# Expert attention on one core: scores in row tiles, maxima on the whole array, keys padded by TensorE, and one unused matmul per unit

## The reference

```python
sx = jnp.einsum('bsh,ndh->bnsd', x, hl_w) + hl_b[None, :, None, :]
q = jnp.einsum('bnsd,neod->bneso', sx, wq)
k = jnp.einsum('bnsd,nod->bnso', sx, wk)
v = jnp.einsum('bnsd,nod->bnso', sx, wv)
scores = jnp.einsum('bnesd,bntd->bnest', q, k) * d ** 0.5 + causal
att = jax.nn.softmax(scores, axis=-1)
qkv = jnp.einsum('bnest,bntd->bnesd', att, v)
```

## Time and profile before

| | |
|---|---|
| median of 3 runs | 1997.99 us (1995.75 to 2002.71) |
| the profiled execution's own time | 2006.71 us |
| its span, first to last instruction | 2004.9 us |
| mean granted TensorE clock | 0.865 |
| busy: PE, PEld, DVE | 86%, 67%, 74% |
| busy: ACT, POOL | 38%, 34% |
| expert attention, first set-up instruction to the last row's update of the stream | 557 us to about 1382 us |
| a turn of its loop (one row, four units) | 24.2 us from 897.34 to 921.53 us |

### The profile page before, as it was taken

The page is one execution under the profiler, slowest core; times in us unless marked ns, Lnnn a source line. Parts: engine busy times, 40 slices in busy tenths (PEclk is TensorE's granted clock), DMA queues, the critical chain, the costliest instruction groups (busy, mean ns, idle before and its releaser), DMA issues. The chain is left out here.

```text
span 2004.9 us, 45616 instructions
## 1 busy us (share of the span) xinstructions
PE 1719.6 (86%) x15064; PEld 1344.4 (67%) x15064; DVE 1488.5 (74%) x4423; ACT 756.6 (38%) x2274; POOL 690.5 (34%) x957
## 2 busy tenths in 40 slices
PE   1499999999769999999999999973999999788887
PEld 1266666666557777777777777752888888677776
DVE  6166676666627898888889888875766665688887
ACT  2245454545324444344344444321222222343442
POOL 2622222222134555545545445532211111322221
PEclk9999999999869999999999999985555555788788
DMA  2000000000000000000000000000000000000000
GB/s 114 1 2 0 0 0 0 0 0 0 1 1 1 1 2 0 0 0 0 0 0 0 0 0 0 1 1 0 1 0 0 0 0 1 1 5 8 4 6 11
DMA packets 6980, 8.13 MB, mean 4 GB/s; under 512 B 6272, under 2 KB 6272, under 8 KB 6784
## 3 DMA queue, kind: packets, MB, share of 16 engines
q1 hardware_dynamic: 6912, 7.25, 1.1%
HBM read 5.71 MB, written 1.54 MB: 4 GB/s over the span
## 5 line engine op out<-in xcount | busy, mean ns | idle before, releaser
L1142 ACT ACTIVATE ex_pT<-ex_T 128x376 f32<-128x376 f32 (+1 forms) x384 | 162.8, 440 | 217.1 <-PE ex_T L1044 207.9
L604 ACT ACTIVATE al_prob<-al_S,al_negmax 94x94 f32<-94x94 f32 (+1 forms) x512 | 146.2, 375 | 180.0 <-DVE al_negmax L731 180.0
L1207 DVE TENSOR_REDUCE ex_negmax<-ex_R 94x2 bf16<-94x376 f32 (+1 forms) x384 | 186.8, 543 | 30.6 <-PE ex_R L1015 30.0
L1044 PE MATMUL ex_T<-ex_qm,ex_kpad 128*128 128x188 f32 x1024 | 189.7, 329 | 0.0
L505 PE MATMUL al_S<-al_kpad,al_qT 128*94 128x376 f32 x384 | 166.5, 516 | 0.0
L1044 PEld LDWEIGHTS ex_T<-ex_qm,ex_kpad 128*128 128x128 f32 x1024 | 163.0, 192 | 5.1
L944 POOL TENSOR_SCALAR_AFFINE_SELECT ex_pT<-ex_pT 128x512 f32<-128x512 f32 x128 | 84.3, 659 | 236.5 <-ACT ex_pT L1142 236.5
L682 POOL TENSOR_TENSOR al_kpad<-al_kT,al_quad_mask 128x1504 f32<-128x1504 f32 x32 | 86.2, 2692 | 186.3 <-ACTq L619 186.3
L731 DVE TENSOR_REDUCE al_negmax<-al_S 94x2 f32<-94x376 f32 (+1 forms) x192 | 99.1, 542 | 62.6 <-PE al_S L506 56.7
L1554 POOL TENSOR_TENSOR ta_kk<-ta_ext 94x320 f32<-94x320 f32 x64 | 60.4, 961 | 246.4 <-DVE ta_qkn L1734 163.0
L1027 PE MATMUL ex_R<-ex_sxT,wsb 128*128 128x188 f32 x256 | 72.3, 364 | 47.5 <-DVE ex_negmax L1207 47.5
(11 more groups left out here) (308 smaller groups left out, 4300.8 us busy)
## 6 DMA issues: line engine op xcount, KB each, us to landing
tok_xin<-x_t SPq DMA_DIRECT2D x4, 760.0 KB, 6.9
wsb<-weights SPq DMA_DIRECT2D x1, 2531.0 KB, 14.2
out<-stream SPq DMA_DIRECT2D x16, 94.0 KB
tok_par<-tok_w SPq DMA_DIRECT2D x1, 4.5 KB, 1.7
```

Source lines behind the costliest of these rows:

```text
L604: last = nc.scalar.activation(p[:, k, cols], S[0:P, k, cols], ACT.Exp, bias=negmax[g % 2][:, m:m + 1])
L1044: last = nc.tensor.matmul(T[:, k, (j % 2) * N:(j % 2 + 1) * N], kpad[par][:, j, 0:K0], qm[e % 2][:], start=True, stop=True)
L1142: nc.scalar.activation(pT[e % 2][rows, k, cols], T[rows, k, cols], ACT.Exp)\
L1207: red(dst, src, AX.X, ALU.max, negate=True).then_inc(sem["r_used"], 1)
```

## The change

All of it is in `expert_attention`. It has these parts.

1. **Scores in row tiles.** `scores` no longer reads padded keys. Each head's matmul uses only its own 32 rows of the array (`tile_position=(32 * n, 0)`), and each head has a bank of `T`, which has four banks now. It is called for heads 0 and 1 and then for heads 2 and 3, and ACT takes one exponential for each pair (2 x 248 elements, `PAIR`) where it took three.
2. **Maxima on the whole array.** `max_scores` takes 128 and 60 queries in place of 94 and 94. The first 128 need keys 0 to 127 only; the last 60 stand twice, in two column tiles of 64, two heads each. `R` has two banks, and `maxima` is two reductions (512 and 376 elements) instead of three of 376. It is issued for the unit after next, where it was for the next.
3. **Queries in T.** `queries` accumulates in bank 0 of `T` (`QCOL`).
4. **Padded keys by PE.** POOL's `kpad` and `kpadb` go; `kpadb` is made by four more matmuls per row with padded weights `ewkb` (two fills, `kb01` and `kb23`), copied out by ACT.
5. **One unused matmul per unit.** `keep_busy(FILLERS)` multiplies 128 x 128 by 128 x 512 in bf16 into `R` before `max_scores`, and nobody reads it; ahead of units 0, 8 and 20 of the run there are 16 more.
6. **Order.** The order of `FILLS` changes, `fg` standing before `sx` now; DVE's body is reordered, with `maxima(rf, 1)`, `mask_values(ru, 2)` and the gate's softmax at its end; POOL's set-up has 34 operations where it had 21.

```diff
+    WARM, WARM_AT = 16, (0, 8, 20)
+    FILLERS = 1
...
-        FILLS = [("xT", FRONT), ("znT", MLP), ("sx", FRONT), ("k", FRONT), ("fc1", MLP), ("pickA", TAIL),
-                 ("fg", LAST), ("q01", FRONT), ("pickB", TAIL), ("q23", FRONT), ("v", FRONT), ("fc2", MLP)]
+        FILLS = [("xT", FRONT), ("znT", MLP), ("fg", LAST), ("sx", FRONT),
+                 ("pickA", TAIL), ("kb01", FRONT), ("kb23", FRONT), ("q01", FRONT),
+                 ("pickB", TAIL), ("fc1", MLP), ("k", FRONT),
+                 ("q23", FRONT), ("v", FRONT), ("fc2", MLP)]
...
-                    if e == 1 and valid(r):
-                        pool.wait_ge(sem["kT_ready"], r + 1)
-                        for dst in (kpadb, kpad):
-                            nc.gpsimd.tensor_tensor(dst[1 - u][:], kT[:].unsqueeze(1).broadcast_to([128, NH, N]),
...
+            def padded_keys(which):
+                return [(X[:, i * N:(i + 1) * N], ewkb[:, n, :], sxb[:]) for i, n in enumerate(which)]
+            def keep_busy(n):
+
+                for _ in range(n):
+                    nc.tensor.matmul(R[:, 0, :], w_parts[:, 0, 0:128], w_parts[:, 0, 128:640], start=True, stop=True)
...
+                need(pe, sem["r_used"], 2 * u)
+                if isinstance(u, int) and u in WARM_AT:
+                    keep_busy(WARM)
+                keep_busy(FILLERS)
+                early = R[:, 0, :].rearrange("p (n s) -> p n s", n=NH)
+                nc.tensor.matmul(early, qTb[par][:, e, 0:K0], kpadb[par][:, :, 0:K0], start=True, stop=False)
+                nc.tensor.matmul(early, eye[:], maskA[:].unsqueeze(1).broadcast_to([128, NH, K0]), start=False, stop=True)\
+                    .then_inc(sem["r_full"], 1)
+                late = R[:, 1, 0:PAIRED * N].rearrange("p (j s) -> p j s", j=PAIRED)
+                for c in range(2):
+                    nc.tensor.matmul(late[QB * c:QB * c + QB], qTb[par][:, e, K0:NP], kpadb[par][:, c::2, :],
+                                     start=True, stop=False, tile_position=(0, QB * c), skip_group_check=True)
...
-                        if k < 2:
-                            last = nc.tensor.matmul(T[:, k, (j % 2) * N:(j % 2 + 1) * N], kpad[par][:, j, 0:K0],
-                                                    qm[e % 2][:], start=True, stop=True)
...
+                for s in range(2):
+                    for n in heads:
+                        rows = slice(32 * n, 32 * n + 32)
+                        if s == 0:
+                            last = nc.tensor.matmul(T[:, n, 0:N], kT[par][rows, 0:K0], qm[e % 2][rows, :], start=True,
+                                                    stop=True, tile_position=(32 * n, 0), skip_group_check=True)
...
+                nc.scalar.activation(pT[e % 2][:, 2:4, :], T[:, 2:4, 0:PAIR], ACT.Exp).then_inc(sem["tB_used"], 1)
...
+                        ins = nc.scalar.activation(pT[e % 2][:, 0:2, :], T[:, 0:2, 0:PAIR], ACT.Exp)
```

More of the change, by code:

```diff
@@ L1032, in queries, with scores @@
-                last.then_inc(sem["m_full"], 1)
-            def scores(r, par, e):
+                for c in range(2):
+                    last = nc.tensor.matmul(T[:, 0, QCOL + K0:QCOL + N], negmaxB[e % 2][:, 32 - 32 * c:160 - 32 * c],
+                                            eye[:, QB * c:QB * c + K1], start=False, stop=True, skip_group_check=True)
+                return last
+            def scores(r, par, e, heads):
                 u = r * NE + e
                 if e == 0:
-                    pe.wait_ge(sem["kpad_ready"], 2 * r + 2)
+                    pe.wait_ge(sem["k_used"], r + 1)
@@ L1039, in scores @@
                 pe.wait_ge(sem["m_used"], u + 1)
[L1040 to L1049 removed]
+                if heads[0] == 0:
+                    pe.wait_ge(sem["tA_used"], u + 1)
+                else:
+                    need(pe, sem["tB_used"], u)
@@ new lines, in scores @@
+                for s in range(2):
[4 more added lines that the diff above has]
+                                                    stop=True, tile_position=(32 * n, 0), skip_group_check=True)
+                        else:
+                            last = nc.tensor.matmul(T[:, n, N:PAIR], kT[par][rows, QB:NP], qm[e % 2][rows, K0:N],
+                                                    start=True, stop=True, tile_position=(32 * n, 0),
+                                                    skip_group_check=True)
@@ L1108, in body @@
                         fill(t, "sx", [(X[:, 0:N], w("hl_t", C), xT[:])])
-                    if e == 1 and valid(rt):
-                        pe.wait_ge(sem["o_used"], NE * (rt + 1))
-                        fill(t, "pickA", picks(odd, slice(0, P)))
-                    if e == 2 and valid(rt):
-                        fill(t, "pickB", picks(odd, slice(P, N)))
+                    if e == 1 and valid(rf):
+                        fill(t, "q01", projections((0, 1)))
+                    if e == 2 and valid(rf):
+                        fill(t, "k", [(X[:, 0:N], w("ewk"), sxT[odd][:, 0:N])])
                     if e == 3 and valid(rm):
@@ new lines, in body @@
+                    if e == 0 and valid(rf):
+                        act.wait_ge(sem["sx_full"], rf + 1)
+                        need(act, sem["o_used"], NE * (rf - 1))
+                        for dst in (sxT[odd][:, 0:N], sxb[:]):
+                            used("sx_used", dst, ALL, slice(0, N), ACT.Identity, bias=w("hl_bt"))
+                    if e == 1 and valid(rf):
+                        act.wait_ge(sem["q01_full"], rf + 1)
+                        used("q01_used", qTb[odd][:, 0:2, 0:N], ALL, slice(0, 2 * N))
@@ L1334, in body @@
                     link(tt(row_halves(rl), row_halves(rl), fout[:], ALU.add))
+                if valid(rf):
+                    maxima(rf, 1)
                 if valid(ru):
                     mask_values(ru, 2, par)
+                if valid(rt):
+                    dve.wait_ge(sem["gexp_ready"], rt + 1)
+                    flat = gate_exp[:].rearrange("p h n e -> p (h n) e")
+                    link(red(top[:], flat, AX.X, ALU.add))
+                    link(nc.vector.reciprocal(top[:], top[:]))
+                    tt(gate[:].rearrange("p h n e -> p (h n) e"), flat,
+                       top[:].unsqueeze(2).broadcast_to([P, HALVES * NH, NE]), ALU.mult).then_inc(sem["gs_ready"], 1)
             dve.wait_ge(sem["consts"], CONSTS)
```

371 lines of the change are left out of this document (180 added, 191 removed).

## The result

The changed kernel takes 2037.8 us (median of 4 runs, 2034.0 to 2045.4), the kernel before 1999.9 beside it: ratio 1.020, 95% interval 1.016 to 1.023, so it is slower, by about 2%. The profiled execution took 2039.1 us, its span 2037.1. The forecast was 2015, a loss of 17 us.

The account below looks back on a forecast made before the run. The bound was taken to be the loop of dependences through PE, DVE and POOL, not one engine. 2006.7 + 16 (steady rows) + 1 (ends) = 2024 us profiled, 8.7 less for the median: 2015, range 1945 to 2050.

Parts of the forecast that it names:

- Scores: PE's scores of one unit in row tiles: 1.0 us instead of 1.92, bounds 0.70 and 1.92.
- The stall at line 1271: DVE's small `tensor_scalar`, 3.22 us until POOL's padding ends: falls to 0.2 us, DVE gains 3.0 us per row.
- The loop of a row: Dependences from POOL's mixing round to the next, through DVE and PE: 23.0 us against 24.1.
- step 1: DVE ends softmax, POOL mixes, DVE sums, does `maxima(2)`, mask and gate operations; PE's `sx` waits for this: 5.0 us.
- steps 2 and 3: PE's `sx`, scores, `pickA` until DVE reads it, 2.4 us; then DVE's pick through PE's maxima to `pickB`, 5.1 us.
- Step 3: DVE picks, PE waits before `kb01`, then maxima, `weigh`, `q01`, scores, `pickB` and hops: 5.1 us.
- Step 4: `queries`, exponential, POOL's masks and power: 5.2 us with hops; DVE's own path about 4 us, so DVE waits for POOL.
- 4 and 5: The loop's last two parts: `queries` through POOL's power, 5.2 us; DVE from normalisation through `maxima(1)` and a mask, 5.3 us.
- The clock: Steady rows: PE idles at waits and the granted clock dips to 0.88, adding 1.6 us per row; chance 0.45.
- The sum: Some 26 steady rows +16 us, ends +1, on 2006.7: 2024 profiled, 8.7 less for the median, 2015 us.
- the ends: POOL's set-up +4.6 us, three bursts +5, first six rows -9: together +1, within 8 either way.
- The rival on the other side: Clock stays full through the unused matmul and bursts: loop 23.0 us, 1970 us, bounds 1950 to 1992; chance 0.36.

Follow-up runs that it names:

- e7: Kernel before the change, with POOL's padding of the keys cut to two columns: 1987 us.
- e6: Changed kernel without its three bursts of 16 unused matmuls, with ten more unused matmuls per row where TensorE waits for VectorE: 1954.9 us.
- e3: Changed kernel with ten more unused matmuls per row inside TensorE's waits (before xT, sx and kb01), bursts kept: 1964.5 us.
- e10: e6 with four unused matmuls ahead of each unit's maxima (16 per row) and none in the waits: 2012 us.
- e11: e6 with its ten unused matmuls in the waits but none ahead of the units' maxima: 1955 us.
- e12: e6 with the ten unused matmuls in the waits using 32 of the array's 128 rows, same 512 columns: 2016.7 us.
- e13: e6 with one more VectorE multiplication of z by norm_g per row, right behind the first one, on the loop: 35 us slower.

## Why the prediction came out as it did

- **Scores** (taken 1.0, bounds 0.70 and 1.92): 0.70, the lower bound; two pairs run as close as four tiles. By the TensorE page of the Trainium skill ("TensorE: Matmul & The Clock Gate", Part 3) the estimate was 1.92 / 3.07 = 0.63; the trace shows 1.92 / 0.70 = 2.7 times.
- **The stall at line 1271**: gone, 0.17 us. That DVE gains these 3 us and the row doesn't, as forecast ("it doesn't, because of what is behind what"), e7 shows from the other side.
- **The loop of a row**: 23.0 forecast, 22.4 with scores of 0.70, 22.1 measured in e6. Step by step it was 5.0, 2.4, 5.1, 5.2, 5.3 against 5.2, 2.5, 5.6, 3.9, 4.9. The terms of step 1 add up to 5.1 even without its hops. With scores of 0.70 the forecast of steps 2 and 3 is 2.1 and 4.8. Step 3 lacked the `queries` of the next unit, which PE does in front of `pickB` (some 0.5 us); they also stand in front of `kb01`, where the forecast wait isn't found. Step 4 was wrong: POOL's power ends as DVE gets to it (922.93 and 922.96 us in e6), and DVE's own 4 us count. Steps 1 to 3 are 1.4 us too short in all, 4 and 5 1.7 too long: that the sum comes so near is luck.
- **The clock**, where the prediction failed in size. The mechanism was right: PE waits at `xT` and `sx`, and the clock goes to its lower level in every row. The term that failed is the one for the clock, 0.24 x 6.6 = +1.6 us per row; measured is +3.2 (25.3 against e6's 22.1). Two steps are in it. The clock was taken as 0.88, 24% of the time low, from the mixture's 0.85; it was 0.82, 36%, and with this share the same product gives 2.4. The other 0.8 is left to the second step, spreading the slow time evenly over the row. The fall comes at the wait, and the waits stand where PE is on the loop, so the slow stretch of the long row (1063 to 1075) is the very one in which `xT`, `queries`, the maxima, `sx`, the scores and `pickA` are waited for. DVE's 1.80, 1.16 and 2.85 us of waits are this; at the same places e6 has none, none and 1.48.
- **The sum.** Steady rows lost 1.2 us each (25.32 against 24.16) where 0.6 was forecast: that is the +32 us of the two `hx` lines against the +16. The two errors work against each other: the loop at full clock came out 0.9 below the forecast 23.0, the clock's term 1.6 above. The start gave +9.4, as forecast (4.6 and 5), but by luck: 8.6 of it were the bursts, and hardly a part was POOL's set-up. By the sixth row it had been made up (785.2 against 785.4), so the ends came to 0 where +1 was forecast.
- **The rival on the other side**, "the clock stays full, because the unused matmul and the bursts keep it so", priced at 1970: it didn't happen here, since neither stands in the waits. Where matmuls do stand there (e3), 1964.5 us came out, near the price and within its bounds of 1950 to 1992.

## What to carry to other kernels

A change that takes work off TensorE in a kernel with a loop through other engines can open waits. Here the clock then fell just where the loop needs TensorE; price such a stretch at half speed, not at the mean. Where the clock had to be held, whole-array matmuls did it inside the waits, right ahead of the instruction that waits; ahead of work that is ready they did little. Test a supposed loop with one extra instruction on it and the same one beside it.

## What the runs showed of the hardware

- The place of unused work decides what it does for the clock: 16 matmuls per row ahead of ready work gave 0.92 and 2012 us, 10 in the waits 0.99 and 1955 us (e10 and e11).
- Ten matmuls per row on 128 rows of the array, beside the four of the units, held the clock at 1.00 (e6, 1954.9 us); ten of the same length on 32 rows, with PE 97% busy, gave 0.89 (e12, 2016.7 us).
- TensorE was given 2.1 us more to do in each row, and the kernel became 3.6% faster (e3 and the changed kernel: 1964.5 and 2037.8 us).
- Near the point where the clock holds, small additions are dear: 0.42 us of DVE work per row, 14 us in 31 rows with its step, cost 35 us. Rows without a fall account for 22 of them, the falls of the clock for the other 13 (e13).
